# New places for the filling stages of an attention block, a second copy of x transposed, and layer norm outputs on GpSimd

## The chip, the cores and the metric

The kernel runs on one core of a Trainium2 chip. The metric is device time in microseconds of one execution; lower is better. TensorE runs at one of two granted clock levels (2.4 GHz, shown as 1.00, and 1.2 GHz, shown as 0.50).

## What is computed

For 16 batches of 512 tokens of width 128, all in float32:

```python
x = layernorm(x + attention(x))      # 16 heads of 8, causal softmax; heads 0 to 2 reweight a third of the tokens by 1.6
x = layernorm(x + ffn(x))            # 256 -> 512 -> 512 -> 128, weights +1 or -1, relu * 2 between, scales s0, s1, s2
```

The softmax subtracts each row's true maximum, so scores are formed twice: once to find the maxima, once (transposed, with the maximum in extra rows of the product) for the exponentials.

## The kernel before

The work is a software pipeline written out by hand. `iteration(n)` runs on every engine for n from -2 to 17. It has four groups `g` of ten steps `t`, written (g, t) here. In each step TensorE forms one 512-column piece of masked scores of batch n (`scores`, L837, into `score_ps`), ScalarE takes its exponential (`exp`, L510, into `e`), and TensorE forms one piece of scores for a later quarter of batch n or n+1 (`max_scores`, L811, into a ring of three PSUM banks `max_ps`), which VectorE reduces to row maxima (`take_max`, L636). `max_scores` waits for `max_taken` of the piece three before it, `scores` for the exponential two before it. In steps 1, 3, 5 and 7 of a group TensorE multiplies the masked exponentials of the group before with v (`sums`, L861, pieces kt 0, 1, 3, 2); the first, second and fourth wait for the causal masks that GpSimd applies (`mask`, L411, pieces 0, 1, 2). ScalarE copies the sums out in step 9 of the group (`sums_out`, L519).

All other products of a batch use two PSUM banks `bank_ps` in turn, in the order of the table `PLACES` (L46). A row has the name, the batch relative to n, the step of the product on TensorE and the step in which ScalarE or VectorE takes it out. `claim` (L799) waits until the user before last of the bank has been taken out, so the order of the table is a chain. The names: `xT` is x transposed, `q`, `k` and `v` the projections, `tok_0` to `tok_3` turn the sums back to tokens (VectorE divides them, `normalise`), `attnT` and `proj` the output projection, `x1T` the first layer norm's result transposed, `ffn0_m`, `ffn1_m` the feed-forward tiles, `ffn2T` and `ffn2` its last product and the transposition back, `rowmax0` and `rowmax1` the maxima of one half of the heads transposed.

Feed-forward products are done as high part plus low part. ScalarE writes the relu to `full` (two slots, in turn, freed by `split_ready`), and GpSimd makes the high part (a cast) and the low part (a subtraction) for `ffn0_m` and `ffn1_m` (`high_and_low_part`, L427); VectorE does so for `x1T` and for all tiles of the last batch. q and k are split in three bfloat16 parts: GpSimd `split` 0, ScalarE's copy in `MIDDLE_STEP`, GpSimd `split` 2. SyncE then copies the parts into the 72 rows of `stack`, nine DMAs for each half of the heads (`stack_half`), once the scores that read the old contents are done. ScalarE's queue adds the three rows of maxima (`rowmax_rows`, L539).

A layer norm takes VectorE's `bn_stats` right behind the residual sum (L712), `bn_aggr` and two small operations in `LN_VAR` (L715), GpSimd's reciprocal root and shift (`rstd_of`, L435), and ScalarE's four scaled copies in `LN_OUT` (L530). `x1T` waits for the latter.

Every engine has its own list of steps in order. GpSimd's is written out in `iteration` (L470 to L494).

Of the kernel before, what the change touches and what calls it, by code (L numbers as in the profile page):

```python
# [58 lines left out]
    ("tok_3", -1, (1, 6), (1, 6)),
    ("ffn2T", -2, (1, 8), (2, 0)),  # L60
    ("ffn2", -2, (2, 2), (2, 3)),
    ("attnT", -1, (2, 3), (2, 3)),
    ("proj", -1, (2, 6), (2, 6)),
    ("x1T", -1, (3, 2), (3, 2)),
    ("rowmax0", 1, (3, 3), (3, 4)),
    ("ffn0_0", -1, (3, 5), (3, 5)),
    ("ffn0_1", -1, (3, 5), (3, 5)),
    ("ffn0_2", -1, (3, 8), (3, 8)),
    ("ffn0_3", -1, (3, 9), (3, 9)),
# [3 lines left out]
FFN2_STEPS = ((1, 8), (1, 8), (1, 9), (1, 9))  # L73

HIGH_STEPS = {"ffn1_0": (0, 4), "ffn1_1": (0, 5), "ffn1_2": (0, 7), "ffn1_3": (1, 3),
              "x1T": (3, 3), "ffn0_0": (3, 5), "ffn0_1": (3, 6), "ffn0_2": (3, 9), "ffn0_3": (3, 9)}

MIDDLE_STEP = (1, 5)

NEGMAX_SPLIT = (((3, 0), (3, 0), (3, 1), (3, 2)), ((1, 0), (1, 0), (1, 1), (1, 2)))  # L80

NEGMAX_ROWS = ((3, 5), (1, 5))

LN_VAR = ((2, 7), (2, 3))
LN_OUT = (((3, 0), (3, 0), (3, 0), (3, 0)), ((2, 7), (2, 7), (2, 7), (2, 7)))
# [25 lines left out]
def block_kernel(nc, x, w_qkv, b_qkv, w_proj, b_proj, k0, k1, k2, s0, s1, s2, out):  # L111
    B, S, D = x.shape
    H, R = HEADS, D // HEADS
    P = 128
# [30 lines left out]
    with ExitStack() as ctx:  # L145
# [18 lines left out]
        one = sb("one", [1, P])  # L164
        exp_one = sb("exp_one", [1, 1])
        wc = sb("wc", [P, 3 * D])
# [15 lines left out]
        xT = sb("xT", [P, S])  # L182
# [30 lines left out]
        w0_half = e[0][:, 5, :]  # L213
        minus_ones = e[1][:, 0, :].bitcast(BF16)[0:3, 0:S]
# [28 lines left out]
        hi_ready = sem("hi_ready")  # L243
# [19 lines left out]
        def ahead(n, g):  # L263

            return (n, 3) if g == 0 else (n + 1, g + -1)
# [11 lines left out]
        def _(sp):  # L277
            sp.dma_start(x_in[:], x_tok[0]).then_inc(x_loaded, 16)
            sp.dma_start(wc[:], w_qkv).then_inc(w_loaded, 16)
# [66 lines left out]
            def iteration(n):  # L346
                later_half(n)
                b = n + 3
                if live(b):
                    wait_full(sp, use_of(b + -1, "xT"))  # L350
                    sp.dma_start(x_in[:], x_tok[b.times(1)]).then_inc(x_loaded, 16)
                earlier_half(n)
                if live(n + -2):
                    store(n + -2)
                if live(n):
                    if n.c > 0:
                        wait_free(sp, use_of(n + -1, "proj"))
                    sp.dma_start(x_res[:], x_tok[n.times(1)]).then_inc(xres_loaded, 16)

# [5 lines left out]
        def _(pool):  # L365
# [61 lines left out]
            def high_and_low_part(b, layer, m):  # L427
                k = 1 + FT * layer + m
                wait_free(pool, use_of(b, f"ffn{layer}_{m}"))
                nc.gpsimd.tensor_copy(h_hi[layer][:, m, :], full[:, full_slot(b, k), :]).then_inc(hi_ready, 1)  # L430
                pool.wait_ge(hi_ready, b.times(9, k + 1))
                nc.gpsimd.tensor_tensor(h_lo[layer][:, m, :], full[:, full_slot(b, k), :],  # L432
                                        h_hi[layer][:, m, :].bitcast(F32), ALU.subtract).then_inc(split_ready, 1)

            def rstd_of(b, i):  # L435
# [5 lines left out]
                                        ALU.mult).then_inc(rstd_ready[i], 1)  # L441

            def iteration(n):
                def low(layer, m):
                    b = n + (-2 if layer else -1)
# [15 lines left out]
                def rstd_of_layer(i):  # L461
                    b = n + (-2 if i else -1)
                    if live(b):
                        rstd_of(b, i)
# [556 lines left out]
```

## Time and profile before

| | |
|---|---|
| Three runs | 995.96, 1007.99, 1011.67 us; median 1007.99 |
| The profiled execution | 994.16 us; span 992.4 us |
| Mean granted clock | 0.928 |
| Busy: TensorE, VectorE, ScalarE, GpSimd | 864.0, 671.9, 605.0, 502.6 us |

The profile has, for each engine, busy time and the idle time before each instruction with what ended it. All terms of the prediction are made against the profiled execution. A span of 992.4 us holds 16 iterations with score steps, which take about 55 us each once the pipeline is full, a head of 73 us before the first score and a tail without scores.

### The profile page before, as it was taken

The numbers are of one execution on the slowest core, as the hardware profiler recorded it, in microseconds if no ns is written. First come the engines' busy times: TensorE is split into PE (matmuls) and PEld (weight loads), VectorE is DVE, ScalarE is ACT, GpSimd is POOL, SyncE is SP. The second block draws the span as 40 slices with busy tenths as digits, with TensorE's granted clock in tenths as the row PEclk, the third lists the DMA queues.
The fourth block names the chain that finished last, engine by engine and source line by source line (L and its number), as shares of the span: only waits on it lengthen the run. The fifth ranks groups of instructions, "written<-read, shape, count | busy, mean of one in ns | idle before, by whom it ended". The sixth has DMA issues, their size and how long they took to land.

```text
span 992.4 us, 17320 instructions
## 1 busy us (share of the span) xinstructions
PE 864.0 (87%) x5824; PEld 439.0 (44%) x5824; DVE 671.9 (68%) x2784; ACT 605.0 (61%) x1106; POOL 502.6 (51%) x625
## 2 busy tenths in 40 slices
PE   2349698999999899989999998989999898999866
PEld 1114244545454454545454453545455454535343
DVE  3367578575867768595967669595857769694234
ACT  2106467566766667576757667576756767576733
POOL 1103145637564654647574664646565655547540
PEclk8558899979999997999999799999989999999887
DMA  3653635345453534455443435455443425300000
GB/s 77 68 76 60 71 51 69 45 71 56 52 63 46 74 45 66 53 71 60 53 63 45 66 45 75 49 71 59 57 54 50 70 34 73 38 23 2 23 11 11
DMA packets 66142, 53.19 MB, mean 54 GB/s; under 512 B 4518, under 2 KB 64006, under 8 KB 66054
## 3 DMA queue, kind: packets, MB, share of 16 engines
q1 hardware_dynamic: 65190, 51.30, 40.2%
q8 instruction: 47, 0.77, 0.4%
q10 hardware_dynamic: 864, 0.79, 0.3%
q14 instruction: 41, 0.34, 0.2%
HBM read 9.24 MB, written 4.19 MB: 14 GB/s over the span
## 4 chain that ended last, share of the span: by engine, by line
PE 51%; DVE 23%; POOL 9%; ACT 5%; DMA 5%; issue 4%; SPq 2%; ACTq 1%; POOLq 0%; DVEq 0%
PE av_ps L882 10%; DVE max_ps L643 10%; PE max_ps L825 10%; PE score_ps L849 8%; PE bank_ps L909 5%; POOL h_lo L432 5%; PE bank_ps L910 5%; PE bank_ps L808 4%; PE bank_ps L955 3%; DMA stack<-rowmaxT 3%; DVE stats L712 3%; POOL h_hi L430 2%; DMA stack<-parts 2%; DVE rowmax L643 2%; PE bank_ps L944 2%
## 5 line engine op out<-in xcount | busy, mean ns | idle before, releaser
L643 DVE CUSTOM_DVE_ANT_0 max_ps<-max_ps,future 128x512 f32<-128x512 f32 (+3 forms) x1024 | 480.3, 514 | 232.7 <-PE max_ps L825 229.6
L516 ACT ACTIVATE e<-score_ps 128x512 f32<-128x512 f32 x640 | 365.1, 595 | 187.7 <-PE score_ps L849 184.5
L825 PE MATMUL max_ps<-stack 72*128 72x512 bf16 (+3 forms) x1024 | 260.5, 318 | 59.9 <-DVE rowmax L643 36.1
L849 PE MATMUL score_ps<-stack 75*128 75x512 bf16 (+3 forms) x1024 | 253.8, 310 | 20.8 <-DMA stack<-rowmaxT 16.1
L423 POOL TENSOR_SCALAR_AFFINE_SELECT e<-e 128x512 f32<-128x512 f32 x256 | 160.2, 646 | 129.7 <-ACT e L516 129.7
L882 PE MATMUL av_ps<-e,vaug 128*9 128x512 f32 (+3 forms) x2048 | 194.3, 453 | 3.1 <-ACT avT L523 1.7
L825 PEld LDWEIGHTS max_ps<-stack 72*128 72x128 bf16 x1024 | 83.5, 101 | 218.0 <-DVE rowmax L643 98.3
L432 POOL TENSOR_TENSOR h_lo<-full,h_hi 128x512 fp32r<-128x512 f32 x120 | 153.4, 1278 | 10.0
L508 ACT ACTIVATE full<-bank_ps,scales 128x512 f32<-128x512 f32 x128 | 86.8, 687 | 114.3 <-PE bank_ps L910 93.1
L643 DVE DVE_READ_ACCUMULATOR2_ANT rowmax<- 128x1 f32 x1024 | 143.2, 140 | 0.0
L849 PEld LDWEIGHTS score_ps<-stack 75*128 75x128 bf16 x1024 | 90.1, 100 | 78.7 <-issue 23.8
L437 POOL TENSOR_TENSOR rstd<-var_eps,minus_half 128x4 f32<-128x4 f32 x32 | 32.5, 1015 | 151.0 <-DVE var_eps L722 151.0
L909 PE MATMUL bank_ps<-h_hi,w 128*128 128x512 f32 x256 | 106.5, 416 | 2.0 <-POOL h_lo L432 1.7
L430 POOL CAST h_hi<-full 128x512 fp32r<-128x512 f32 x120 | 73.0, 609 | 65.0 <-ACT full L508 65.0
L910 PE MATMUL bank_ps<-h_lo,w 128*128 128x512 f32 x256 | 101.1, 395 | 0.0
L406 POOL TENSOR_TENSOR qk<-qk,parts 128x1024 f32<-128x1024 f32 x15 | 31.9, 2127 | 122.5 <-ACT qk L508 122.5
L882 PEld LDWEIGHTS av_ps<-e,vaug 128*9 128x9 f32 x2048 | 31.2, 88 | 86.4 <-issue 79.7
L534 ACT ACTIVATE res<-res,shift,rstd 128x128 f32<-128x128 f32 x128 | 52.5, 483 | 15.0 <-POOL shift L440 15.0
L909 PEld LDWEIGHTS bank_ps<-h_hi,w 128*128 128x128 f32 x256 | 48.3, 189 | 20.8 <-POOL h_lo L432 6.1
L910 PEld LDWEIGHTS bank_ps<-h_lo,w 128*128 128x128 f32 x256 | 48.5, 189 | 8.7
L808 PE MATMUL bank_ps<-ident,avT 128*128 128x128 f32 x256 | 40.2, 280 | 3.3 <-ACT qk L508 2.6
L955 PE MATMUL bank_ps<-xT,wqk 128*128 128x512 f32 x64 | 38.6, 690 | 2.1 <-ACT xT L508 0.8
(83 smaller groups left out, 791.6 us busy)
## 6 DMA issues: line engine op xcount, KB each, us to landing
stack<-parts SPq DMA_DIRECT2D x288, 128.0 KB
x_in<-in_L_attn_hidden_states SPq DMA_DIRECT2D x16, 256.0 KB, 5.7
x_res<-in_L_attn_hidden_states SPq DMA_DIRECT2D x16, 256.0 KB, 11.4
out_x<-res SPq DMA_DIRECT2D x16, 256.0 KB, 10.9
stack<-rowmaxT ACTq DMA_DIRECT2D x32, 24.0 KB
e<-in_L_ffn_k SPq DMA_DIRECT2D x1, 256.0 KB, 3.5
wc<-in_L_attn_c_attn_w SPq DMA_DIRECT2D x1, 192.0 KB
e<-in_L_ffn_k SPq DMA_DIRECT2D x1, 128.0 KB, 3.3
```

The lines of the kernel that those rows point to most:

```text
L423: last = nc.gpsimd.affine_select(out=ap, in_=ap, compare_op=ALU.is_ge, fill=0.0, base=0, pattern=[[0, 4], [1, P]], channel_multiplier=-1)
L430: nc.gpsimd.tensor_copy(h_hi[layer][:, m, :], full[:, full_slot(b, k), :]).then_inc(hi_ready, 1)
L432: nc.gpsimd.tensor_tensor(h_lo[layer][:, m, :], full[:, full_slot(b, k), :], h_hi[layer][:, m, :].bitcast(F32), ALU.subtract).then_inc(spl ...
L508: nc.scalar.activation(out_ap, bank_ps[:, u[0], :], func, **kw).then_inc(bank_free[u[0]], 1)
L516: nc.scalar.activation(e[g % 2][:, t, :], score_ps[:, t % 2, :], ACT.Exp, scale=SCALE).then_inc(exped, 1)
L643: return nc.vector.tensor_tensor_reduce(out=scored_block, in0=scored_block, in1=future[:, P * (T - 1 - qt):S], scale=1.0, scalar=NEG, op0= ...
L808: last = nc.tensor.transpose(bank[:, P * i:P * i + P], src, ident[:])
L825: return nc.tensor.matmul(out_ap[:, col:col + width], st[0:QK_ROWS, h, 0, P * qt:P * qt + P], st[0:QK_ROWS, h, 1, 0:width], start=True, st ...
L849: return nc.tensor.matmul(out_ap[:, col:col + width], st[0:ALL_ROWS, h, 1, P * kt:P * kt + P], st[0:ALL_ROWS, h, 0, P * kt:S], start=True, ...
L882: last = nc.tensor.matmul(av_ps[32 * j:32 * j + R + 1, P * kt:S], vaug[b.parity][:, kt, G * g + j, :], src, start=(order == 0), stop=(orde ...
L909: nc.tensor.matmul(bank, w, hi, start=(i == 0), stop=False)
L910: last = nc.tensor.matmul(bank, w, lo, start=False, stop=(i == len(pairs) - 1))
```

## The change

The table `PLACES` and the step tables beside it are new: `xT`, `q` and `k` of batch n+2 move to group 0, `ffn2T` and `ffn2` to group 0, `tok`, `attnT` and `proj` to group 1, `x1T` and two of the `ffn0` tiles to group 2, the others and two of the `ffn1` tiles to group 3. `xT` has two buffers. The second copies of the layer norm are four GpSimd `tensor_scalar` operations in place of four of ScalarE, and the statistics have steps of their own. The high parts of `ffn0_2` and `ffn0_3` are cast by VectorE. GpSimd's list is rewritten. SyncE waits for `rowmax0` of batch n+1 before it loads `x_res` and stores the output. `max_steps` replaces `ahead`; with both its tables empty it gives the same one step of the max pass beside each score step. `wc` is split into two loads.

```diff
 PLACES = (
-    ("ffn1_0", -2, (0, 4), (0, 4)),  ("ffn1_1", -2, (0, 4), (0, 4)),  ("ffn1_2", -2, (0, 6), (0, 6)),
-    ("v", 1, (0, 7), (0, 8)),        ("ffn1_3", -2, (0, 9), (0, 9)),  ("xT", 2, (0, 9), (0, 9)),
-    ("q", 2, (1, 0), (1, 1)),        ("k", 2, (1, 1), (1, 2)),        ("tok_0", -1, (1, 2), (1, 2)),
-    ("tok_1", -1, (1, 3), (1, 3)),   ("rowmax1", 0, (1, 4), (1, 4)),  ("tok_2", -1, (1, 5), (1, 5)),
-    ("tok_3", -1, (1, 6), (1, 6)),   ("ffn2T", -2, (1, 8), (2, 0)),   ("ffn2", -2, (2, 2), (2, 3)),
-    ("attnT", -1, (2, 3), (2, 3)),   ("proj", -1, (2, 6), (2, 6)),    ("x1T", -1, (3, 2), (3, 2)),
-    ("rowmax0", 1, (3, 3), (3, 4)),  ("ffn0_0", -1, (3, 5), (3, 5)),  ("ffn0_1", -1, (3, 5), (3, 5)),
-    ("ffn0_2", -1, (3, 8), (3, 8)),  ("ffn0_3", -1, (3, 9), (3, 9)),
+    ("xT", 2, (0, 0), (0, 0)),       ("ffn1_2", -2, (0, 0), (0, 1)),  ("ffn1_3", -2, (0, 2), (0, 3)),
+    ("q", 2, (0, 3), (0, 4)),        ("k", 2, (0, 4), (0, 5)),        ("ffn2T", -2, (0, 5), (0, 7)),
+    ("v", 1, (0, 7), (0, 8)),        ("ffn2", -2, (0, 9), (0, 9)),    ("tok_0", -1, (1, 0), (1, 0)),
+    ("tok_1", -1, (1, 2), (1, 2)),   ("rowmax1", 0, (1, 3), (1, 3)),  ("tok_2", -1, (1, 4), (1, 4)),
+    ("tok_3", -1, (1, 5), (1, 5)),   ("attnT", -1, (1, 7), (1, 7)),   ("proj", -1, (1, 9), (2, 0)),
+    ("x1T", -1, (2, 6), (2, 6)),     ("ffn0_0", -1, (2, 8), (2, 8)),  ("ffn0_1", -1, (2, 9), (2, 9)),
+    ("ffn0_2", -1, (3, 0), (3, 1)),  ("ffn0_3", -1, (3, 1), (3, 3)),  ("rowmax0", 1, (3, 3), (3, 4)),
+    ("ffn1_0", -1, (3, 6), (3, 7)),  ("ffn1_1", -1, (3, 8), (3, 9)),
 )
-MIDDLE_STEP = (1, 5)
-LN_VAR = ((2, 7), (2, 3))
-LN_OUT = (((3, 0), (3, 0), (3, 0), (3, 0)), ((2, 7), (2, 7), (2, 7), (2, 7)))
+FFN2_STEPS = ((0, 5), (0, 5), (0, 6), (0, 6))
+HIGH_ON_POOL = ("ffn0_0", "ffn0_1", "ffn1_0", "ffn1_1", "ffn1_2", "ffn1_3")
+MIDDLE_STEP = (0, 8)
+NEGMAX_ROWS = ((3, 5), (1, 4))
+LN_STATS = ((2, 1), (3, 5))
+LN_VAR = ((2, 2), (3, 6))
+MAX_TWICE = ()
+MAX_NONE = ()
...
-            xT = sb("xT", [P, S])
+            xT = [sb(f"xT{i}", [P, S]) for i in range(2)]
...
                 earlier_half(n)
-                if live(n + -2):
-                    store(n + -2)
+                if live(n + 1):
+                    wait_free(sp, use_of(n + 1, "rowmax0"))
                 if live(n):
...
                     sp.dma_start(x_res[:], x_tok[n.times(1)]).then_inc(xres_loaded, 16)
+                if live(n + -2):
+                    store(n + -2)
...
+                pool.wait_ge(rstd_ready[i], b.times(2, 2))
+                x = res2 if i else res1
+                for t in range(T):
+                    ins = nc.gpsimd.tensor_scalar(x[:, t, :], x[:, t, :], rstd[:, i, t:t + 1], shift[:, i, t:t + 1],
+                                                  ALU.mult, ALU.add)
+                ins.then_inc(ln_step[i], 1)
...
+                low(1, 1); low(1, 2); low(1, 3); masks(0, 0); split_qk(0); masks(0, 1); split_qk(2); masks(0, 2)
+                bias_residual(); masks(1, 0); masks(1, 1); layernorm_out(0); masks(1, 2); masks(2, 0)
+                low(0, 0); low(0, 1); masks(2, 1); low(0, 2); masks(2, 2); low(0, 3); masks(3, 0)
+                layernorm_out(1); low(1, 0); masks(3, 1); masks(3, 2)
```

The table and GpSimd's list are folded here to several entries a line. `low(1, 0)` belongs to batch n-1 and the other `low(1, m)` to n-2. The steps at which VectorE takes high parts follow the new places (`x1T` in (2, 7), `ffn0_2` in (3, 2), `ffn0_3` in (3, 3)).

## Rows read from the trace of the kernel before

**Rows 1.** Windows of one iteration each: length, busy time and count by engine

```profile
312.33:367.22 54.89, 51.21 (x366) 26.42 (x365) 41.10 (x173) 37.40 (x70) 32.17 (x40) 1.00 0.48 59
367.22:424.63 57.41, 54.78 (x366) 28.53 (x365) 40.94 (x173) 38.00 (x70) 32.69 (x40) 0.91 0.45 57
```

**Rows 2.** Windows of groups 0, 1, 2 and 3 of one iteration

```profile
393.57:411.24 17.67, 17.31 (x113) 10.53 (x112) 10.29 (x40) 10.67 (x21) 14.65 (x19) 1.00 0.52 60
411.24:425.27 14.03, 13.71 (x96) 6.91 (x97) 10.13 (x45) 9.72 (x18) 8.10 (x8) 1.00 0.28 31
425.27:436.10 10.83, 9.47 (x81) 4.84 (x81) 9.60 (x44) 8.23 (x17) 2.90 (x5) 1.00 0.54 65
436.10:448.51 12.41, 10.90 (x80) 4.56 (x80) 11.66 (x50) 9.30 (x20) 6.09 (x10) 1.00 0.61 87
```

**Rows 3.** Timeline of TensorE in that iteration: start, length, instruction, idle before

```profile
403.59 0.48 PE L909 MATMUL bank_ps<-h_hi,w 128*128 128x512 f32 x1
...
405.54 0.39 PE L825 MATMUL max_ps<-stack 72*128 72x384 bf16 x2
...
428.11 0.38 PE L825 MATMUL max_ps<-stack 72*128 72x512 bf16 x1
...
436.10 0.38 PE L825 MATMUL max_ps<-stack 72*128 72x512 bf16 x1 [1.36 <-DVE rowmax L643]
...
437.30 0.39 PE L825 MATMUL max_ps<-stack 72*128 72x512 bf16 x1 [0.60 <-DVE rowmax L643]
...
439.57 0.66 PE L808 MATMUL bank_ps<-ident,res 128*128 128x128 f32 x4 [0.15 <-ACT res L534]
...
443.30 0.47 PE L909 MATMUL bank_ps<-x_hi,w 128*128 128x512 f32 x1 [0.34 <-DVE x_lo L732]
```

**Rows 4.** Timeline of VectorE in that iteration

```profile
428.53 0.70 DVE L643 CUSTOM_DVE_ANT_0 max_ps<-max_ps,future 128x512 f32<-128x512 f32 x1
...
429.14 0.69 DVE L756 TENSOR_TENSOR res<-bank_ps,res 128x512 f32<-128x512 f32 x1
429.87 0.87 DVE L712 BATCH_NORM_STATS2 stats<-res 128x6 f32<-128x128 f32 x4
...
431.34 0.56 DVE L643 CUSTOM_DVE_ANT_0 max_ps<-max_ps,future 128x384 f32<-128x384 f32 x1
...
442.46 0.69 DVE L732 TENSOR_TENSOR x_lo<-full,x_hi 128x512 fp32r<-128x512 f32 x1
```

**Rows 5.** Timeline of GpSimd in that iteration

```profile
431.51 1.02 POOL L437 TENSOR_TENSOR rstd<-var_eps,minus_half 128x4 f32<-128x4 f32 x1 [5.15 <-DVE var_eps L722]
432.61 0.20 POOL L440 TENSOR_TENSOR shift<-neg_mean,rstd 128x4 f32<-128x4 f32 x1
...
445.85 0.61 POOL L430 CAST h_hi<-full 128x512 fp32r<-128x512 f32 x1 [3.70 <-ACT full L508]
446.54 1.27 POOL L432 TENSOR_TENSOR h_lo<-full,h_hi 128x512 fp32r<-128x512 f32 x1
...
449.68 1.23 POOL L423 TENSOR_SCALAR_AFFINE_SELECT e<-e 128x512 f32<-128x512 f32 x2
```

**Rows 6.** Timeline of ScalarE in that iteration

```profile
420.93 1.06 ACT L596 ACTIVATE parts<-qk 128x1024 bf16<-128x1024 f32 x1 [0.53 <-issue]
...
425.02 0.59 ACT L523 ACTIVATE avT<-av_ps 128x512 f32<-128x512 f32 x1
```

**Rows 7.** Groups of instructions by line: a one-input GpSimd operation of 128 columns

```profile
L377 POOL TENSOR_SCALAR_AFFINE_SELECT ident<-ident 128x128 f32<-128x128 f32 x1 | 0.3, 292 | 0.2 <-POOL e L373 0.2
```

**Rows 8.** Timeline of SyncE's queue: the nine stack copies of a half

```profile
424.63 6.03 SPq L310 DMA_DIRECT2D stack<-parts  x9
```

**Rows 9.** The chain that ended last, in order of time: start, length, what

```profile
109.72 10.41 DMA stack<-rowmaxT
...
950.27 0.70 ACT full L508
...
957.68 1.14 PE bank_ps L967 x8
```

More of the change, by code:

```diff
@@ L61 @@
[L61 to L64, printed above, removed]
+    ("xT", 2, (0, 0), (0, 0)),
+    ("ffn1_2", -2, (0, 0), (0, 1)),
+    ("ffn1_3", -2, (0, 2), (0, 3)),
+    ("q", 2, (0, 3), (0, 4)),
+    ("k", 2, (0, 4), (0, 5)),
+    ("ffn2T", -2, (0, 5), (0, 7)),
+    ("v", 1, (0, 7), (0, 8)),
+    ("ffn2", -2, (0, 9), (0, 9)),
+    ("tok_0", -1, (1, 0), (1, 0)),
+    ("tok_1", -1, (1, 2), (1, 2)),
+    ("rowmax1", 0, (1, 3), (1, 3)),
@@ L65 @@
+    ("tok_2", -1, (1, 4), (1, 4)),
+    ("tok_3", -1, (1, 5), (1, 5)),
+    ("attnT", -1, (1, 7), (1, 7)),
+    ("proj", -1, (1, 9), (2, 0)),
+    ("x1T", -1, (2, 6), (2, 6)),
+    ("ffn0_0", -1, (2, 8), (2, 8)),
+    ("ffn0_1", -1, (2, 9), (2, 9)),
+    ("ffn0_2", -1, (3, 0), (3, 1)),
+    ("ffn0_3", -1, (3, 1), (3, 3)),
     ("rowmax0", 1, (3, 3), (3, 4)),
[L66 to L69, printed above, removed]
+    ("ffn1_0", -1, (3, 6), (3, 7)),
@@ L70 @@
+    ("ffn1_1", -1, (3, 8), (3, 9)),
 )
 BANK_USES = tuple((what, batch) for what, batch, _, _ in PLACES)
[L73 to L84 removed]
@@ L85 @@
-LN_OUT = (((3, 0), (3, 0), (3, 0), (3, 0)), ((2, 7), (2, 7), (2, 7), (2, 7)))
+FFN2_STEPS = ((0, 5), (0, 5), (0, 6), (0, 6))
+HIGH_STEPS = {"x1T": (2, 7), "ffn0_0": (2, 9), "ffn0_1": (3, 0), "ffn0_2": (3, 2), "ffn0_3": (3, 3),
+              "ffn1_0": (3, 7), "ffn1_1": (3, 9), "ffn1_2": (0, 1), "ffn1_3": (0, 4)}
+HIGH_ON_POOL = ("ffn0_0", "ffn0_1", "ffn1_0", "ffn1_1", "ffn1_2", "ffn1_3")
+MIDDLE_STEP = (0, 8)
+NEGMAX_SPLIT = (((3, 0), (3, 0), (3, 1), (3, 2)), ((0, 9), (1, 0), (1, 1), (1, 2)))
+NEGMAX_ROWS = ((3, 5), (1, 4))
@@ L261, in wait_free, with max_steps @@
             eng.wait_ge(bank_free[u[0]], u[1])
-        def ahead(n, g):
-            return (n, 3) if g == 0 else (n + 1, g + -1)
+        def max_steps(n, g, t):
+            each = [2 if (g_, t_) in MAX_TWICE else 0 if (g_, t_) in MAX_NONE else 1
+                    for g_ in range(G) for t_ in range(STEPS)]
+            first = sum(each[:STEPS * g + t])
+            for i in range(first, first + each[STEPS * g + t]):
+                quarter = i // STEPS
+                b = n + 1 if quarter else n
+                if live(b):
+                    yield b, (quarter + 3) % G, i % STEPS
+        highs_of_dve = [w for w in HIGH_STEPS if w not in HIGH_ON_POOL]
+        HIGHS_OF_DVE = len(highs_of_dve)
         def last_batch(b):
@@ L737, in iteration @@
                     for t in range(STEPS):
-                        b, quarter = ahead(n, g)
-                        if live(b):
-                            take_max(b, quarter, t)
+                        for b, quarter, step in max_steps(n, g, t):
+                            take_max(b, quarter, step)
                         for what, d, _, step in PLACES:
@@ L943, in fill_bank @@
                     for kt in range(T):
[L944 to L945 removed]
+                        last = nc.tensor.matmul(bank[:, P * kt:P * kt + P], xT[b.parity][:, P * kt:P * kt + P],
+                                                wv[:], start=True, stop=True)
                     last.then_inc(bank_full[u[0]], 1)
@@ L981, in iteration @@
                     for t in range(STEPS):
-                        b, quarter = ahead(n, g)
-                        if live(b):
-                            max_scores(b, quarter, t)
+                        for b, quarter, step in max_steps(n, g, t):
+                            max_scores(b, quarter, step)
                         if live(n):
```

134 lines of the change are left out of this document (59 added, 75 removed).

## The prediction

> **What bounds the kernel now.** I read the windows of single iterations first. Once the pipeline is full an iteration takes 54.9 us, and TensorE is busy for 51.2 us of it, VectorE for 41.1, ScalarE for 37.4, GpSimd for 32.2 [rows 1]. TensorE is the engine to follow, and only its idle 3.7 us can be won; the work on it is moved by the change, not removed. Where a stretch at the lower clock falls in an iteration (0.91 granted over 57.4 us, so some 10 us at 1.2 GHz) it takes 57.4 us instead [rows 1]; that is every third iteration.
>
> Then the windows of the four groups: 17.7, 14.0, 10.8 and 12.4 us [rows 2]. VectorE is busy for 9.6 and 11.7 us of the last two and TensorE idle for 1.4 and 1.5 us. The timeline of TensorE shows what for [rows 3]: 1.36 and 0.60 us at the start of group 3, waiting for row maxima, since VectorE does both layer norms' sums, statistics and variances in group 2. The other waits are small: 0.15 us for ScalarE's layer norm output, 0.34 for the low part of x1, and five of 0.15 to 0.27. The named waits come to 3.5 us an iteration. Measured from start to start, as I measure below, they are 4.9, because a wait also drains the array and reloads weights; the work proper is then 50.0 us.
>
> **The change, part by part.** Work of TensorE per group after the change, in start-to-start times: ten score and ten max pieces, sums and their changeovers 7.4 us; an `ffn1` tile 1.95 (403.59 to 405.54, [rows 3]), `ffn2T` 1.9, `q`, `k`, `v`, `proj` about 1.0 each, every set of four transposes 0.45, an `ffn0` tile 0.5. That gives 17.4, 11.1, 8.9 and 12.6 us for groups 0 to 3, sum 50.0 as before. VectorE gets 9.4, 10.3, 10.7 and 11.1: it is over TensorE in group 2 alone, by less than the three pieces that it may lag. So the 1.36 + 0.60 us go. What is late next has to be walked through. I put T = 0 at the end of the first max piece of group 2.
>
> *Layer norm to `x1T`.* `proj` is at the end of group 1, so VectorE starts its first piece at 0.2 (0.42 behind TensorE, 428.11 to 428.53, [rows 3, 4]), the residual sum 0.61 later [rows 4], a max piece, statistics (0.8), a max piece, aggregation and the two small ones (0.57 between max pieces). GpSimd's root starts at 4.2, as it starts 0.17 before VectorE's next piece now (431.34 and 431.51, [rows 4, 5]). Root and shift take 1.3 with their waits [rows 5], to 5.5. Four copies follow. GpSimd's price for a scaled copy of 128 columns is in no row: the nearest is a one-input operation of 128 columns, 0.29 us [rows 7]; a quarter of its 512-column cast is 0.15 (0.61 for all, [rows 5]), a quarter of its subtraction 0.32 (1.27) and, with a fixed part added, 0.46. I take 0.3, ends 0.15 and 0.46. Ready at 6.9, ends 6.3 and 7.5. TensorE comes to `x1T` at 5.2 (six pairs of pieces at 0.45, sums 0.98 + 0.76 + 0.34, changeovers). **It waits 1.7 us**; now it waits 0.15, since `x1T` stands six steps later. The mask (1, 2) is behind the copies on GpSimd, ready at 7.6, in time for its sums.
>
> The Trainium skill, page "GPSIMD Engine Reference", section "Elementwise — side-by-side cycle accounting", says that one-input work is bound by the port at 1.03 cycles a column and two-input work at about 2.6, and its selection table keeps elementwise work on VectorE. It speaks against this edit. The two rows agree in kind (0.61 against 1.27 us for 512 columns). By its one-input figure alone, an estimate, four copies would take 0.45 us plus dispatch and `x1T` would wait about 1 us.
>
> *`x1T` to `ffn0_0`.* With `x1T` at S, VectorE's piece (2, 7) ends at S + 1.6, high part and low part take 0.45 to 0.85 and 0.69 [rows 4], to S + 2.8 to 3.2. TensorE has two pieces and 0.55 us of sums until then, and comes at S + 2.0. **It waits 1.0 us** (0.34 now). `ffn0_0` starts at U = 10.0.
>
> *Masks behind low parts.* GpSimd starts the high part of `ffn0_0` 1.6 us behind its first product and needs 1.9 us for each of two tiles (445.85 to 446.54 to 447.8, [rows 5]), to U + 5.4, then mask (2, 1), 1.23 us [rows 5], to U + 6.65. TensorE comes to the sums that need it at U + 5.5. **It waits 1.2 us**; in the old order the masks of group 3 are not needed until a group later. The two casts given to VectorE (0.4 to 0.85 each) are hidden: TensorE's group 3 has 1.5 us more work than VectorE's. Without that cover they cost their length. They take 1.2 us from GpSimd, which is why `ffn1_0` finds its last low part in time (U + 9.75 against U + 11).
>
> *Bank of `ffn1_1`.* ScalarE takes it out behind an exponential and the sums copy (0.59, [rows 6]), 2.25 us after its last product; TensorE comes to `ffn1_2`, the next user of the bank but one, after 1.35. **0.9 us.**
>
> *`tok_0`.* It needs the last sums copy, in (0, 9). ScalarE does exponential, `MIDDLE_STEP` copy (1.06, [rows 6]), exponential and sums copy from 0.65 to 3.1 after the piece (0, 8) starts; TensorE has two pairs and `ffn2` until 1.8. **1.4 us**; now there are three steps between.
>
> Taking eight scaled copies from ScalarE (3.3 us) frees an engine that waits for scores; nothing on the path, worth 0 to 0.15. Two buffers of x transposed take away a wait for `v` that the new order would have; no wait of that kind is in the rows. Earlier q and k splits give SyncE nothing, since its copies wait for the scores that read the stack. The added wait for `rowmax0` holds `x_res` and the store, which nobody needs for 20 us, and the next half's stack copies behind them, which wait for the scores of step (3, 9) anyhow: 0.
>
> Sum: 1.7 + 1.0 + 1.2 + 0.9 + 1.4 = 6.2, and 0.3 of small ones, against 4.9: an iteration of 56.5 us, 1.6 longer. Unsure by 0.3 at each of five waits, and by 1.4 if the busy column (51.2) is the better measure of work: 55.3 to 58.0. It counts for the 14 iterations with older batches behind them: +22 us.
>
> *Ends.* Without max pieces the last scored iteration has more in it than before (two `ffn1` tiles more, and TensorE outruns the layer norm and the low parts): +6. The tail before has four `ffn1` tiles ahead of `tok_0`, until 950.3, and 34.7 us from `proj` at 957.7 to the end [rows 9]. After, `tok_0` comes some 12 us behind the last scores, not 19, and `ffn2T` is ahead of it: -9. Head: the first scores wait for the same copies; -1. The stretches at the lower clock cost 2.5 us now and at most 5.2 (half of 10.3) if they fall on TensorE's work alone: +2 in all. Total 992.4 + 22 - 4 + 2 = 1012, or 1014 with the 1.8 us around the span. The median of the runs lies 14 us above the profiled execution, the fastest 2 us above. I take 6 us of that: **1020 us**.
>
> **Rivals.** *The waits are absorbed.* If the copies are short and the orders of ScalarE and GpSimd do not meet TensorE as walked, about half of the new waits go. For: every one is a race won or lost by 1 to 2 us. Against: each has its own row. The stack stream sets a floor here: nine copies issued at 424.6 [rows 8] are ahead of the maxima's rows, and where groups 2 and 3 are shorter, in the first scored iteration, those rows take 10.4 us to land [rows 9] and the next scores start 23.4 us after the stream's issue. Groups 2 and 3 take 23.2 now, so at best they stay there. The Trainium skill, page "DMA: Bandwidth & Descriptors", section "Queues, rings and completion order", has the engines take turns between queues packet by packet, by which 24 short rows would not wait for a stream; the 10.4 us say otherwise. Iteration 54 to 55.3: 973 to 1003.
>
> *Faster.* All five waits and the floor fail to show: 51.5 us an iteration, 14 x -3.4 - 2 = -50: 945. More likely partly so, 950 to 975.
>
> *GpSimd's copies are slow.* Its root of four columns takes 1.02 us [rows 5], so an operation can have a fixed price far above its size. At 1 us for each scaled copy `x1T` waits 4.5 us, mask (1, 2) is late too, and the second layer norm holds `low(1, 0)`. It decides from about 0.5 us a copy. Iteration 59.5: 994 + 64 - 4 = 1055.
>
> *The maxima's rows land late.* `x_res` now goes out at the same moment as they do. At 10.4 us [rows 9] instead of some 4 the next scores wait 3.5 us: 1060. Against: the stack stream is nearly over by then.
>
> **Chances.** The forecast, 1003 to 1038: 0.50. Waits absorbed, 975 to 1003: 0.22. Faster, below 975: 0.13. Slow copies or late rows, above 1038: 0.15. What a measurement can tell from no change is about 2%, here 20 us against 994 to 1008. Of the forecast half lies above that. Slower by over 2%: 0.25 + 0.15 + 0.02 = 0.42; faster by over 2%: 0.13 + 0.05 = 0.18; within: 0.40. The range takes in the forecast, the absorbed case and half of each outer one: 972 to 1056.
>
> **What would show it.** Windows of one iteration at 56 to 57 us with TensorE busy for 51; no wait of `max_ps` on VectorE's row maxima at the start of group 3; instead TensorE waiting for GpSimd's `res` (1.7), for `x_lo` (1.0), for `e` masked by GpSimd in group 3 (1.2), for ScalarE's `full` at the start of group 0 and for `avT` at `tok_0`. GpSimd's scaled copy at 0.3 us. It is wrong if the copies cost another size, if a wait that I found is covered by one ahead of it, or if the low clock falls on other work.

## The result, and the profile after

The change makes the kernel slower: 1074.9 us median (1070.5 to 1077.1, 4 runs) against 1004.9 (995.96 to 1011.67, 4 runs) on the same chip, a ratio of 1.071 [1.065, 1.077]. (The table ahead of the prediction has three of these four runs of before; the fourth took 1001.8 us.) That is outside the range of 972 to 1056 us. Ratios and their 95% intervals, here and below, leave out runs of a kernel that fell in a slower state with a lower clock, while medians are of all runs unless the text says otherwise. The profiled execution took 1076.6 us, its span 1074.9, with a mean granted clock of 0.856 where it was 0.928.

The slices of the page show the granted clock of TensorE in 40 equal stretches (the kernel before has most at 9). After the head about every second one stands at 8:

```profile
span 1074.9 us, 17334 instructions
PE 931.3 (87%) x5824; PEld 464.4 (43%) x5824; DVE 691.4 (64%) x2814; ACT 559.0 (52%) x978; POOL 543.0 (51%) x722
PEclk8556598989898898989899898989889898989898
```

The windows of three iterations, to be laid beside [rows 1] (length, busy time and count of TensorE, its weight loads, VectorE, ScalarE, GpSimd, then granted clock, DMA share and GB/s):

```profile
397.64:459.08 61.44, 56.27 (x366) 28.68 (x366) 42.09 (x175) 34.72 (x62) 34.81 (x45) 0.89 0.41 53
459.08:520.50 61.42, 56.25 (x365) 28.64 (x365) 42.04 (x175) 34.67 (x62) 34.80 (x45) 0.89 0.40 53
520.50:581.93 61.43, 56.26 (x365) 28.66 (x365) 42.07 (x175) 34.70 (x62) 34.79 (x45) 0.89 0.39 53
```

Each takes 61.4 us and is at 0.89; before, it was 54.9 at 1.00 and 57.4 at 0.91 in every third. TensorE has the same 366 instructions and is busy for 5 us more: the same matmuls take longer. Windows inside the second of these iterations show where:

```profile
459.84:467.39 7.55, 5.62 (x46) 1.80 (x43) 6.93 (x33) 4.21 (x8) 3.00 (x7) 1.00 0.52 66
467.39:469.30 1.91, 1.91 (x19) 1.16 (x20) 0.99 (x5) 1.09 (x2) 1.13 (x2) 0.99 0.59 55
469.30:479.50 10.20, 9.66 (x29) 3.52 (x28) 4.89 (x18) 4.72 (x8) 4.92 (x6) 0.50 0.52 59
479.50:508.70 29.20, 26.52 (x179) 15.16 (x178) 17.48 (x77) 18.21 (x32) 20.72 (x26) 1.00 0.45 66
508.70:510.20 1.50, 1.49 (x12) 0.87 (x16) 1.50 (x3) 0.70 (x2) 1.50 (x2) 1.00 0.56 67
510.20:513.60 3.40, 3.40 (x15) 1.19 (x15) 3.08 (x10) 1.19 (x2) 1.67 (x2) 0.50 0.03 9
```

Two stretches are at 0.50 (1.2 GHz), 10.2 and 3.4 us long; from 264 us on every iteration has the same two. The timeline of TensorE (start, length, instruction, idle before) tells what stands ahead of each:

```profile
459.84 0.38 PE L844 MATMUL max_ps<-stack 72*128 72x512 bf16 x1
...
467.39 0.66 PE L827 MATMUL bank_ps<-ident,res 128*128 128x128 f32 x4 [1.94 <-POOL res L468]
...
470.34 0.76 PE L928 MATMUL bank_ps<-x_hi,w 128*128 128x512 f32 x1 [0.54 <-DVE x_lo L748]
...
475.80 1.90 PE L901 MATMUL av_ps<-e,vaug 128*9 128x512 f32 x8
...
490.49 0.51 PE L928 MATMUL bank_ps<-h_hi,w 128*128 128x512 f32 x1 [0.88 <-ACT full L537]
...
508.71 0.38 PE L844 MATMUL max_ps<-stack 72*128 72x512 bf16 x1 [1.58 <-DVE rowmax L658]
```

The long stretch begins 1.9 us after TensorE idled 1.94 us for `x1T`, the short one 1.5 us after it idled 1.58 us at the start of group 1. In the first the sums of eight pieces take 1.90 us; at full clock they take 1.05 (649.55 in the trace of the trial with the later `MIDDLE_STEP` below). The waits of 1.36 and 0.60 us at the start of group 3 [rows 3] are gone, as forecast.

GpSimd's timeline of the same iteration, and its group of scaled copies on the page (busy, mean ns of one):

```profile
464.20 1.02 POOL L460 TENSOR_TENSOR rstd<-var_eps,minus_half 128x4 f32<-128x4 f32 x1 [5.27 <-DVE var_eps L737]
465.30 0.20 POOL L463 TENSOR_TENSOR shift<-neg_mean,rstd 128x4 f32<-128x4 f32 x1
465.61 1.73 POOL L468 TENSOR_SCALAR res<-res,rstd,shift 128x128 f32<-128x128 f32 x4
```

```profile
L468 POOL TENSOR_SCALAR res<-res,rstd,shift 128x128 f32<-128x128 f32 x128 | 56.2, 453 | 3.3
```

The root starts 4.0 us after the end of the group's first piece (459.84 + 0.38), the copies end at 7.1, and one costs 0.45 us.

### The profile page after: what moved, and what is told of

Its sections match the earlier page's. It is cut to its first block, busy times and chain, and to the rows that moved or that the text cites. A ratio compares the mean times of both kernels' runs of the same rounds, so it can differ in the third digit from the quotient of the medians.

```text
span 1074.9 us, 17334 instructions
## 1 busy us (share of the span) xinstructions
PE 931.3 (87%) x5824; PEld 464.4 (43%) x5824; DVE 691.4 (64%) x2814; ACT 559.0 (52%) x978; POOL 543.0 (51%) x722
## 4 chain that ended last, share of the span: by engine, by line
PE 68%; DVE 12%; POOL 6%; issue 4%; ACT 4%; DMA 3%; SPq 2%; ACTq 0%; POOLq 0%; DVEq 0%
PE av_ps L901 14%; PE max_ps L844 13%; PE score_ps L868 11%; PE bank_ps L928 9%; PE bank_ps L929 7%; PE bank_ps L827 6%; DVE max_ps L658 4%; POOL res L468 3%; DMA stack<-parts 2%; PE bank_ps L974 2%; POOL rstd L460 2%; PE bank_ps L943 2%; SPq L327 2%; PE bank_ps L986 2%; PE bank_ps L963 2%
## 5 line engine op out<-in xcount | busy, mean ns | idle before, releaser
L545 ACT ACTIVATE e<-score_ps 128x512 f32<-128x512 f32 x640 | 370.2, 597 | 401.4 <-PE score_ps L868 382.2
L844 PE MATMUL max_ps<-stack 72*128 72x512 bf16 (+3 forms) x1024 | 280.1, 338 | 46.0 <-DVE rowmax L658 27.1
L868 PE MATMUL score_ps<-stack 75*128 75x512 bf16 (+3 forms) x1024 | 273.1, 330 | 9.3 <-DMA stack<-rowmaxT 8.5
L901 PE MATMUL av_ps<-e,vaug 128*9 128x512 f32 (+3 forms) x2048 | 215.0, 495 | 0.2 <-POOL e L441 0.2
L844 PEld LDWEIGHTS max_ps<-stack 72*128 72x128 bf16 x1024 | 88.6, 105 | 237.8 <-issue 129.6
L868 PEld LDWEIGHTS score_ps<-stack 75*128 75x128 bf16 x1024 | 95.8, 105 | 52.0 <-issue 18.9
L450 POOL CAST h_hi<-full 128x512 fp32r<-128x512 f32 x90 | 54.9, 610 | 82.0 <-ACT full L537 81.9
L928 PE MATMUL bank_ps<-x_hi,w 128*128 128x512 f32 x64 | 51.4, 804 | 9.5 <-DVE x_lo L748 9.5
L468 POOL TENSOR_SCALAR res<-res,rstd,shift 128x128 f32<-128x128 f32 x128 | 56.2, 453 | 3.3
L827 PE MATMUL bank_ps<-ident,avT 128*128 128x128 f32 x256 | 45.2, 307 | 1.0 <-ACT avT L552 0.6
```

The costliest lines, as they stand in the source:

```text
L468: ins = nc.gpsimd.tensor_scalar(x[:, t, :], x[:, t, :], rstd[:, i, t:t + 1], shift[:, i, t:t + 1], ALU.mult, ALU.add)
L545: nc.scalar.activation(e[g % 2][:, t, :], score_ps[:, t % 2, :], ACT.Exp, scale=SCALE).then_inc(exped, 1)
L827: last = nc.tensor.transpose(bank[:, P * i:P * i + P], src, ident[:])
L844: return nc.tensor.matmul(out_ap[:, col:col + width], st[0:QK_ROWS, h, 0, P * qt:P * qt + P], st[0:QK_ROWS, h, 1, 0:width], start=True, st ...
L868: return nc.tensor.matmul(out_ap[:, col:col + width], st[0:ALL_ROWS, h, 1, P * kt:P * kt + P], st[0:ALL_ROWS, h, 0, P * kt:S], start=True, ...
L901: last = nc.tensor.matmul(av_ps[32 * j:32 * j + R + 1, P * kt:S], vaug[b.parity][:, kt, G * g + j, :], src, start=(order == 0), stop=(orde ...
```

## The experiments

The texts on record call the rivals theories. Theory A: the waits are much as forecast, and most of the loss is the clock, which falls behind idle spots of TensorE that the new order makes in every iteration. Theory B: the low clock comes from the order of the work or from load, not from idle spots. Theory C: the waits alone are the loss. "Products" below are matmuls of constants that nobody reads, of 128 x 512 bfloat16, 0.24 us each; the computation is whole in all kernels.

### Products in both idle spots of the kernel after

```diff
+            def busy(out, k):
+                for _ in range(k):
+                    nc.tensor.matmul(out, ident_bf[:], future[:], start=True, stop=True)
...
                 if what == "x1T":
+                    busy(claim(u), 9)
                     pe.wait_ge(ln_step[0], b.times(4, 4))
...
+                        if (g, t) == (1, 0) and live(n) and live(n + -1):
+                            pe.wait_ge(exped, n.times(G * STEPS, STEPS * g + t - 1))
+                            busy(score_ps[:, t % 2, :], 7)
```

> The changed kernel with idle TensorE time filled by products whose result nobody reads: nine 128x512 bfloat16 products ahead of the wait for x1T (into the bank that x1T then overwrites), seven ahead of the first max piece of group 1. Nothing is taken away; TensorE gets 16 products of 0.22 us more in each iteration. Theory A (the clock falls behind the two waits, and half of the loss is the clock, not the waits): both low stretches go or nearly so, an iteration falls from 61.4 to about 56.5 us, 1075 becomes 1000 to 1020. Theory B (the low clock comes from the new order of the work, its bursts of feed-forward products, or from load alone): the clock stays at 0.86, the time at 1070 to 1085. Theory C (the waits alone are the loss): the products fit into the waits, 1075 unchanged.

Measured: 1023.4 us, ratio 1.016 [1.008, 1.024], clock 0.952. Sixteen matmuls more in each iteration make the kernel 51 us faster (medians, on two chips; the ratios to before fall from 1.071 to 1.016). The page's slices and the windows of two iterations:

```profile
PEclk8557899999999999999999999999999999999897
```

```profile
300.00:357.60 57.60, 53.83 (x384) 28.15 (x380) 43.84 (x174) 34.33 (x62) 34.76 (x45) 1.00 0.43 57
357.60:415.20 57.60, 53.83 (x384) 28.16 (x380) 43.84 (x174) 34.33 (x63) 34.76 (x45) 1.00 0.43 56
```

The iteration falls from 61.4 to 57.6 us, where 56.5 was expected, and the time ends 3 us above theory A's 1000 to 1020. B and C had 1070 us and more, so theory A holds. What is left to before is 57.6 against 54.9 us.

### Products ahead of x1T alone

> The same with the nine products ahead of x1T alone. Theory A: the 10.2 us stretch behind x1T goes and the 3.4 us one in group 1 stays: three quarters of the clock's loss, an iteration of 57.5 to 58.5 us, 1020 to 1040 in all. Theories B and C: 1070 to 1080.

Measured: 1030.0 us, 1.021 [1.014, 1.029], clock 0.942. Stretches of 3.4 us at half clock come in about every second iteration, behind the other spot. The spot ahead of `x1T` is the dear one. That is theory A's forecast, 1020 to 1040.

### Half as many products (4 and 4)

> The kernel after, with 4 products ahead of the wait for x1T and 4 ahead of the first score piece of group 1, in place of 9 and 7: about 1 of the 1.9 us and 0.9 of the 1.6 us are filled. Theory A (it takes an idle spot of over about 1.5 us to bring the clock down, as the run with ScalarE's copies suggests, where 1.78 us did it only now and then): the clock stays up nearly always, iterations of 57.5 us: 1020 to 1032 us, ratio 1.01 to 1.025. Theory B (part of the filling gives part of the gain): 1040 to 1060 us, ratio 1.03 to 1.05, low stretches in about every second iteration.

Measured: 1022.9 us, 1.019 [1.014, 1.025], clock 0.953, iterations of 57.6 us. TensorE still idles 1.08 us for `x1T` and 0.71 at the start of group 1, and behind the head no iteration has a stretch at half clock. The spots need not be closed, only shortened. The time is in theory A's range. Its reason, a spot of over about 1.5 us, can't be the whole one: before has falls behind 1.36 and 0.60 us.

### The same sixteen products where TensorE is busy

They stand ahead of the score pieces (1, 5) and (3, 5).

> The kernel after, with the same sixteen products (7 and 9) ahead of the score pieces (1, 5) and (3, 5), where TensorE is busy, and none at its two idle spots. Theory A (the products help because they fill the idle spots behind which the clock falls): both spots stay, the clock falls as in after, and the products cost up to their length, 3.4 to 3.8 us an iteration: 1095 to 1130 us, ratio 1.09 to 1.12, clock 0.85 to 0.87. Theory B (more work anywhere keeps the clock up): 1010 to 1050 us, clock above 0.92.

Measured: 1098.3 us in the profiled execution (clock 0.906, where 0.85 to 0.87 was expected), 1117.0 to 1125.6 in three others at 0.864 to 0.880. There is no interval; before on the same chip took 1006.0, so the profiled execution alone is at 1.09, the lower end of theory A's range. Work as such doesn't help: the same products in the idle spots gave 1023.4. The profiled execution has iterations of both kinds, which makes it the cleanest measure of the clock in the study:

```profile
275.01:336.08 61.07, 53.74 (x379) 28.26 (x381) 44.21 (x175) 34.51 (x62) 34.86 (x45) 1.00 0.38 54
679.00:743.85 64.85, 59.42 (x380) 30.30 (x381) 42.27 (x175) 34.92 (x62) 34.87 (x46) 0.89 0.38 50
```

64.85 less 61.07 is 3.8 us, as 61.4 less 57.6. The timeline of TensorE in the iteration at full clock shows every wait of the new order undisturbed:

```profile
283.36 0.66 PE L831 MATMUL bank_ps<-ident,res 128*128 128x128 f32 x4 [1.95 <-POOL res L468]
...
286.30 0.47 PE L932 MATMUL bank_ps<-x_hi,w 128*128 128x512 f32 x1 [0.75 <-DVE x_lo L748]
...
292.96 0.83 PE L905 MATMUL av_ps<-e,vaug 128*9 128x384 f32 x8 [1.15 <-POOL e L441]
...
305.34 0.50 PE L932 MATMUL bank_ps<-h_hi,w 128*128 128x512 f32 x1 [0.88 <-ACT full L537]
...
323.55 0.38 PE L848 MATMUL max_ps<-stack 72*128 72x512 bf16 x1 [1.57 <-DVE rowmax L658]
...
328.85 0.39 PE L916 MATMUL bank_ps<-ident_bf,rowmax_parts 128*24 128x128 bf16 x4 [0.68 <-DVE rowmax_parts L687]
```

So an idle spot of 1.95 us did not bring the clock down here, and 1.94 did elsewhere. The wait for `x1T` is followed by a fall in 8 of 13 iterations of this execution, and in all 14 of after.

### The scaled copies back on ScalarE, at (2, 5) and (3, 8)

> The changed kernel with the scaled copies of both layer norms back on ScalarE, in (2, 5) and (3, 8). Theory A: ScalarE's four copies end 1.6 us behind the shift, GpSimd's 1.85 us, so x1T still waits 1.7 us and the clock still falls: 1065 to 1078. Theory D (GpSimd's slower copies, 0.45 us each, are the cause, by delaying x1T and the masks and low parts queued behind them): 1030 to 1050.

Measured: 1040.7 us, 1.030 [1.022, 1.038], clock 0.920. `x1T` waits 1.78 us, so the copies' engine is worth 0.16 us of waiting, as theory A had it; but the time is 34 us lower than after's (medians, on two chips), theory A's 1065 to 1078 is missed and the time lies in theory D's 1030 to 1050. Two iterations of it:

```profile
444.95:502.39 57.44, 50.37 (x365) 26.68 (x365) 43.82 (x175) 37.51 (x70) 31.39 (x37) 1.00 0.42 57
502.39:561.02 58.63, 53.20 (x365) 28.03 (x365) 42.70 (x175) 37.87 (x70) 31.40 (x37) 0.94 0.43 56
```

Undisturbed, the iteration is 57.4 us, against 57.6 with GpSimd's copies and half the products. So theory D's mechanism, later masks and low parts, gives next to nothing; the gain is that the clock falls less often and for less. The wait for `x1T` is followed by a fall in 6 of 14 iterations. Whether that is due to its 0.16 us or to the other differences between the two kernels is not shown: a wait of 1.95 us was followed in only 8 of 13 above. The price of a wait can't be put in proportion to its length.

### The scaled copies on GpSimd alone, in the order of before

The four `tensor_scalar` go behind `rstd_of` and `layernorm_out` leaves ScalarE; nothing else of the change is in.

> One part of the change alone: the kernel before, with both layer norms' scaled copies on GpSimd (four tensor_scalar behind its root and shift) and none on ScalarE. Theory A (the copies are harmless with x1T six steps later; they take 0.45 us each): GpSimd busy for 3.6 us more in an iteration, ScalarE 3.3 less, x1T finds its input ready, nothing on TensorE's path but perhaps 0.3 us; 990 to 1015 us, ratio 0.985 to 1.01. Theory B (GpSimd's list is late by it: masks and low parts behind the copies hold TensorE, or VectorE's casts stretch beside them): new waits of 1 us or more for e or x_lo, and with them the lower clock: 1030 to 1060 us.

Measured: 1001.2 us, 0.997 [0.993, 1.001], clock 0.924. One of the ten runs took 1595.2 us at a mean clock of 1.00; why is open, and the ratio leaves it out. The page's group of the copies, and where they show on TensorE in an undisturbed iteration:

```profile
L445 POOL TENSOR_SCALAR res<-res,rstd,shift 128x128 f32<-128x128 f32 x128 | 55.9, 454 | 3.3
```

```profile
273.03 0.66 PE L809 MATMUL bank_ps<-ident,res 128*128 128x128 f32 x4 [0.33 <-POOL res L445]
```

This edit is harmless where `x1T` stands six steps later. So the copies by themselves are not the loss. In the new places, by the run before this one, having them on GpSimd costs some 34 of the 70 us, nearly all of it by the clock.

### The kernel before, with idle added

TensorE waits for the exponential of its own step at (1, 8) and (1, 9).

> The kernel before, with TensorE made to wait in steps (1, 8) and (1, 9) for the exponential of the same step, about 1 us each: idle time and nothing else, in a group where nothing else is late. Theory A: the clock falls behind them in each iteration: 2 us of waits and 2 to 4 us of clock, 1035 to 1065, mean clock below 0.90. Theories B and C: the waits alone, at most 28 us more, 1005 to 1025, clock as before (0.93).

Measured: 1053.0 and 1064.9 us in the two runs that the ratio counts, 1.050 [1.037, 1.063], in theory A's range; two more took 1079.2 and 1079.3. The profiled execution (1064.9) has clock 0.873. TensorE idles 0.69 us at each of the two places:

```profile
625.58 0.51 PE L924 MATMUL bank_ps<-h_hi,w 128*128 128x512 f32 x1 [0.69 <-ACT e L516]
...
627.93 0.52 PE L924 MATMUL bank_ps<-h_hi,w 128*128 128x512 f32 x1 [0.69 <-ACT e L516]
```

In four iterations the clock falls there, as at 628.3. The spots of 1.36 and 0.60 us at the start of group 3, the same as before, are now followed by a fall in all 13 iterations, where before it was 5. How much of the loss is the waits' own length stays open.

### The kernel before, with eight products ahead of the same two pieces

> The kernel before with four 128x512 products ahead of each of the score pieces (1, 8) and (1, 9), 1.8 us an iteration, at the place where e4 has TensorE idle for about as long. Theory A: the 1.8 us are paid once, 14 to 16 times, and the clock stays as before: 1022 to 1038. If length of the iteration or the place is what made e4 slow, as e4: 1055 to 1075.

Measured: 1040.4 us, 1.032 [1.025, 1.038], clock 0.898, slightly over theory A's 1022 to 1038. An undisturbed iteration takes 56.7 us, the products' length more; the rest is low clock, none of it in group 1, where the idle added in the run before brought it four times, but still behind the waits of 1.36 and 0.60 us at the start of group 3: in 11 of 13 iterations, with the waits themselves as before.

### The kernel before, with products in its own idle spot

```diff
+                        if (g, t) in ((3, 0), (3, 1)) and live(n) and live(n + -1):
+                            pe.wait_ge(exped, n.times(G * STEPS, STEPS * g + t - 1))
+                            busy(score_ps[:, t % 2, :], 5 if t == 0 else 2)
```

> The kernel before with the wait for row maxima at (3, 0) and (3, 1) (1.36 and 0.60 us) filled with five and two 128x512 products into the score bank that the next piece overwrites. Theory A (the clock falls behind idle spots of TensorE): the low stretch in every third iteration, worth 2.5 us each, goes: 10 to 13 us less, ratio 0.985 to 0.995. Theory B (load alone sets it): more products, more low stretches, ratio 1.00 to 1.02.

Measured: **988.7 us, 0.981 [0.976, 0.987]**, clock 0.949, below the expected 0.985. It beats both kernels, before by a difference that the interval shows, though not as one of over 2%. The slices, one iteration, and the spot itself:

```profile
PEclk9557699999999999999999999999999999999987
```

```profile
419.56:474.42 54.86, 52.41 (x373) 27.18 (x372) 41.02 (x173) 37.42 (x70) 32.33 (x40) 1.00 0.49 60
```

```profile
430.82 1.25 PE L801 MATMUL score_ps<-future,ident_bf 128*128 128x512 bf16 x5 [1.17 <-ACT e L516]
431.91 0.38 PE L829 MATMUL max_ps<-stack 72*128 72x512 bf16 x1
```

The products don't begin when TensorE runs dry: they wait 1.17 us for the exponential. So one spot of 1.17 us is left in place of 1.36 and 0.60. The next max piece starts 2.6 us behind the last score piece of group 2, not 1.7, and yet the iteration is still 54.9 us; what goes is every third iteration's 57.4.

### Both sets of products in the kernel before

> The kernel before, with 5 and 2 products ahead of the score pieces (3, 0) and (3, 1) (as in the run at 0.981) and 4 ahead of each of the pieces (1, 8) and (1, 9) (as in the run at 1.032). Theory A (those eight products cost their own length, 1.8 us an iteration, and the rest of the 3.2% was the lower clock behind the idle spot at the start of group 3, which is now filled): iterations of 54.9 + 1.8 = 56.7 us with no stretch at half clock, 989 + 15 x 1.8 = about 1016 us, ratio 1.00 to 1.015, clock 0.95. Theory B (the eight products cost more than their length for a reason of their own, such as a later chain): the two effects add, -1.9% + 3.2%: 1.013 to 1.03 without low clock, iterations of 57.5 us or more.

Measured: 1014.8 us, 1.011 [1.006, 1.016], clock 0.955, iterations of 56.6 us at 1.00. The ratio lies in theory A's range and touches theory B's; the iterations (56.6, not 57.5 or more) decide for A: the eight products cost their length, and the rest of the 3.2% was the clock behind the start of group 3. With products there the kernel with more work is some 2% faster (1.011 against 1.032). A spot of 1.40 us is left there in each iteration, and no fall follows it:

```profile
446.62 1.03 PE L801 MATMUL score_ps<-future,ident_bf 128*128 128x512 bf16 x4 [1.40 <-DVE rowmax L643]
```

### What holds TensorE at the start of group 1

The forecast had ScalarE's `avT` behind its `MIDDLE_STEP` copy. Both trials are the first kernel above with one more edit.

```diff
-MIDDLE_STEP = (0, 8)
+MIDDLE_STEP = (0, 9)
```

> The kernel with both idle spots filled (e1) as base, so that the clock plays no part, and MIDDLE_STEP moved from (0, 8) to (0, 9), behind ScalarE's sums copy in the same step. ScalarE then has the last sums copy 1.0 us earlier. If the wait at the start of group 1 is the forecast's (tok_0 for that copy behind the middle copy), an iteration falls by up to 1 us, 15 us in all (1008). If it is the ring of max_ps (40 pieces a batch are no multiple of 3, so that the first piece of a batch needs the bank of the piece right before it, and VectorE is late there because of v), nothing moves: 1018 to 1028.

Measured: 1081.3 us, 1.064 [1.052, 1.075], outside both expectations. The ratio counts runs of 1065.3 and 1080.7 us; the trace is of one of 1082.0. Undisturbed iterations take 58.8 us. Timelines of TensorE, VectorE and GpSimd:

```profile
645.09 0.38 PE L848 MATMUL max_ps<-stack 72*128 72x256 bf16 x2
...
648.15 0.38 PE L848 MATMUL max_ps<-stack 72*128 72x512 bf16 x1
...
654.64 0.39 PE L916 MATMUL bank_ps<-ident_bf,rowmax_parts 128*24 128x128 bf16 x4 [1.86 <-DVE rowmax_parts L687]
```

```profile
648.46 2.03 DVE L681 CAST rowmax_parts<-rowmax 128x32 bf16<-128x32 f32 x1
```

```profile
648.33 2.13 POOL L426 TENSOR_TENSOR parts<-qk,parts 128x1024 bf16<-128x1024 f32 x1 [2.79 <-ACT parts L611]
```

`avT` ends 1 us earlier, at 647.3, yet from piece (0, 8) to the first piece of group 1 it is 3.06 us as in after (505.65 to 508.71). That looks as if it was not `avT`, but the trial can't tell: the base's seven products stand ahead of this piece and end at 648.08, so nothing could have made it start earlier. The edit pushed GpSimd's split onto VectorE's cast of the maxima, which took 2.03 us, and TensorE waits 1.86 us for the maxima's parts; the low clock returns in several iterations.

The second trial moves `v` ahead of `ffn2T`:

```diff
-    ("ffn2T", -2, (0, 5), (0, 7)),
-    ("v", 1, (0, 7), (0, 8)),
+    ("v", 1, (0, 5), (0, 6)),
+    ("ffn2T", -2, (0, 6), (0, 8)),
```

> The same base with v two steps earlier on TensorE and VectorE ((0, 5) and (0, 6)) and ffn2T one step later ((0, 6), (0, 7), out in (0, 8)). If VectorE and the ring of max_ps hold the start of group 1, VectorE is free 1 us earlier there and an iteration falls by up to 1 us, less what ffn2 now waits for ffn2T: 1008 to 1020. If tok_0's sums copy holds it, which the later ffn2T delays: 1025 to 1040.

Measured: 1043.4 us, 1.033 [1.028, 1.039], no low clock, iterations of 58.7 us; outside both expectations. The new place makes `ffn2` wait 0.83 us for ScalarE's `ffn2T`, and (0, 8) to (1, 0) grows to 3.9 us. The seven products stand ahead of this piece too, so this trial doesn't decide either. What does speak is after's timelines: VectorE ahead of that piece, then ScalarE's `avT` and TensorE's `tok_0`:

```profile
506.80 0.69 DVE L706 TENSOR_TENSOR vaug<-bank_ps,bv 128x512 f32<-128x512 f32 x1
507.52 0.26 DVE L710 TENSOR_TENSOR vaug<-vaug,mult 128x96 f32<-128x96 f32 x1
507.70 0.43 DVE L658 CUSTOM_DVE_ANT_0 max_ps<-max_ps,future 128x256 f32<-128x256 f32 x1
508.04 0.14 DVE L658 DVE_READ_ACCUMULATOR2_ANT rowmax<- 128x1 f32 x1
508.04 0.47 DVE L658 CUSTOM_DVE_ANT_0 max_ps<-max_ps,future 128x256 f32<-128x256 f32 x1
```

```profile
508.21 0.60 ACT L552 ACTIVATE avT<-av_ps 128x512 f32<-128x512 f32 x1
```

```profile
509.14 0.60 PE L827 MATMUL bank_ps<-ident,avT 128*128 128x128 f32 x4
```

Both items of `v` stand ahead of the maxima of the pieces (0, 8) and (0, 9), and the ring of three banks lets the first piece of a batch go only when the last piece of the batch before (40 pieces, each batch starting at its first bank) has left the same bank. VectorE is done with it at about 508.5, and the piece starts at 508.71. `avT` is ready at 508.81, 0.1 us later, when TensorE is still at that step's pieces; `tok_0` doesn't wait. Without VectorE's lag TensorE would have come to `tok_0` at about 507.6 and have waited some 1.2 us for `avT` (estimates from these rows). So two waits of nearly the same end lie over one another: the one that shows is VectorE's, and the forecast's stands hidden behind it.

## Why the prediction was wrong

The slower side was its likeliest case, the size was not: the forecast was a span of 1012 us, the measured one 1074.9. The spans of the two filled kernels, which have no stretch at half clock behind the head, split the 82.5 us between the kernels. From before filled (980.9) to after filled (1020.9) it is 40.0 us: the new order. Low clock costs 54.0 in after (1074.9 - 1020.9) and 11.5 in before (992.4 - 980.9), so 42.5 more. Of the 40.0, 14 iterations at 2.7 us are 38, and 2 are the ends. These are single executions, and before's is the fastest on record: by medians the products take 20 us off before (1008.8 to 988.7) and 51 off after, so that some 31 us are left for the difference in low clock. The forecast was made against the execution with little of it.

- **The step that failed is the last of the ends**: "The stretches at the lower clock cost 2.5 us now and at most 5.2 ... +2 in all". It measured +42.5. I had taken the one stretch of before's third iteration as a given and asked only on what work it falls. It depends on the idle spots, and how often it follows one changes with the rest of the kernel: of the 63 us that the span exceeds the forecast, 40 are this.
- **The sum of the waits was right.** Forecast 1.7, 1.0, 1.2, 0.9 and 1.4 us, sum 6.2; undisturbed 1.95, 0.75, 1.15, 0.88 and 1.57, sum 6.3. The fifth has another cause in part, see `tok_0`. The 1.36 and 0.60 us at the start of group 3 went. One wait was not seen: 0.68 us for the maxima's parts, because VectorE's cast of them now lies beside GpSimd's work. The iteration is 57.6 us against 56.5, +2.7 in place of +1.6: 0.7 is that wait, 0.1 the others; the last 0.3 is not settled. Times 14 it is 16 us.
- **The scaled copy** was priced at 0.3 us with 0.46 as upper end; it is 0.45. GpSimd's root came 0.2 us earlier than walked, so `x1T` was ready at 7.1, not 6.9, and TensorE came to it at 5.2 as walked. The estimate from the one-input figure of the Trainium skill, page "GPSIMD Engine Reference", section "Elementwise — side-by-side cycle accounting" (0.45 us plus dispatch for all four), was further off: four took 1.73. The 0.45 to 0.85 us for VectorE's high parts stands in no row of [rows 4]; before's groups by line have them at 0.66 us (`x1T`) and 0.42 us on average, and the group with the two new ones has a mean of 0.51 in after and 0.86 in the kernel with half the products. Whether that is the 0.3 us left open above is not tested.
- **`tok_0`** had the right size, but the wait that shows is another. TensorE stops at the max piece just ahead of `tok_0`, for VectorE's maxima of the ring's last bank, which stand behind its two items for `v`. `avT` would have held it nearly as long. This is read from the timeline; neither trial isolates it.
- **Masks behind low parts** wait 1.15 us at full clock as forecast. In after itself this wait doesn't show: TensorE arrives late enough at half clock.
- **The ends** were forecast at -4 and are +2.
- **The rivals.** Absorbed waits and the faster case did not come, nor did copies of 1 us or the case of late rows at 1060. No rival had the clock, which turned out to be the largest term; the range ended 19 us short for that.

## What to carry to other kernels

Where a tuned kernel keeps TensorE nearly always busy, count its idle spots one by one and not only by sum: a new order with two spots of 1.6 and 1.9 us in each iteration lost more to the clock behind them (3.8 us an iteration) than to the spots themselves. A spot of a given length may be followed by low clock in every iteration of one kernel and in some of those of another, so only the windows' granted clock tells. If a spot can't be removed, fill part of it with products that nobody reads, placed ahead of the wait, and check that the granted clock of the windows goes to 1.00. When a step is moved, walk also what then lies beside it on VectorE and GpSimd, and which piece is the ring's last before a wrap.

## What the runs showed of the hardware

- **TensorE's clock.** Between the head and the last iterations every fall to 0.50 in these traces begins between 0.7 us ahead of the end of an idle spot of 1.35 to 2.0 us and 2.5 us behind it, or at the second of a pair of 0.69 us spots, and the stretch lasts 3.4 to 17 us. Not every such spot is followed by one. The wait of 1.94 us for `x1T` was followed in 14 of 14 iterations of after, and one of 1.95 in 8 of 13 with the products elsewhere. The waits of 1.36 and 0.60 us were followed in 5 of 13 in the kernel before, 11 with eight products in group 1 and 13 with idle added there; a single 1.40 us was followed in none. With after's spots at 1.08 and 0.71 us none followed in any full iteration. What decides between the cases is open. Seven products per iteration took 2% off the kernel before, sixteen took 51 us off the one after.
- **VectorE beside GpSimd.** A cast of 128x32 took 2.03 us while a GpSimd `tensor_tensor` of 2.13 us ran, and ended with it (650.49 and 650.46); in the kernel before its mean is 331 ns. The groups of after by line have it at:

```profile
L681 DVE CAST rowmax_parts<-rowmax 128x32 bf16<-128x32 f32 x32 | 23.3, 728 | 0.1
```

  The Trainium skill, page "SBUF — State Buffer", section "Who interferes with whom", says that a cast on VectorE can enter a mode that contends with GpSimd for a shared port pair, and that the first to issue holds the pair for its whole instruction. The trace agrees with it here: GpSimd's instruction started at 648.33, the cast at 648.46.
- **GpSimd's scaled copy** with two per-partition scalars takes 0.45 us for 128 columns, in either order of the work.
